# Attention, then a masked convolution: denominators of the last image's last four groups summed by TensorE, and the first pair's preparation moved a slot ahead

## The chip, the cores and the metric

The kernel runs on one core of one Trainium2 chip. The metric is the device time of one execution in microseconds; the median of three runs before the change is 2693.74 us (2692.41 to 2695.08).

## The reference

The input x has 8 images of 512 channels and 32 x 32 positions. Two layers follow one another, each with a residual addition. Cut to what matters:

```
# layer 0: attention, 8 heads per channel split of 64, over the normalised input
q, k, v = t @ Wq.T + bq, t @ Wk.T + bk, t @ Wv.T + bv      # t = group norm of x, as tokens
q, k, v = (a.reshape(B * 8, S, 64) for a in (q, k, v))      # 64 groups of 1024 x 64
attn = softmax(q @ k.T / sqrt(64))
x = x + (attn @ v, back in image form)
# layer 1: a 3x3 convolution behind a mask
xn = group norm of x
mu_x, mu_y = rounded centroids of each channel of xn
m = max(1 - (|posX - mu_x| + |posY - mu_y|) * mask_weight, -1)   # 1 where filter != 1
x = x + conv3x3(max(xn * m, 0), weight) + bias
```

## The kernel before, in words

Each engine has its own program, and the order of its work is written out by hand; semaphores tie the programs together. Work of stage 1 (attention) comes in 64 groups, eight per image. A group has one slot, `slot(img, s)`, and a slot has eight units u. The loops run over image and s; the last image (`more=False`) is written out apart.

In unit u of slot s TensorE (PE) does for the group of this slot four score matmuls (`scores`, L655, into three banks), and for the group of the next slot two or three tiles of maxima (`max_tile`, L630), 16 in a slot and none in units 6 and 7. In units 2, 4, 6, and unit 0 of the next slot, it weighs the values with four kernel chunks' exponentials (`weigh_pair`, L667, fp32, two halves of the array side by side). In slots 0 to 2 it has projections too, which use `qk_bank` in slots 0 and 1. The small tiles go through a ring of three banks (`v_ring`, `take`): a fourth tile waits until VectorE (DVE) has read the first. ScalarE (ACT) takes the exponentials (`exp_tile`, L842, two per unit).

The denominators of a softmax are sums over exponentials. Before the change DVE (`add_tile`, L1150, even tiles) and GpSimd (POOL, `add_tile`, L997, odd tiles) each make seven additions of 128x512 per group, and PE sums the two results over partitions with a matrix of ones (`den_item`, L644 and L646) in unit 2 of the next slot. DVE copies the bank to `den_sb` (L1182); two small transfers, a reciprocal and two more transfers bring back the reciprocals, and POOL multiplies (`divide`, unit 6) and adds the residual (`residual`, unit 7). `exp_tile` waits for the additions that still read its buffer (`sum0`, `sum1`).

Stage 2 (convolution) handles images in four pairs. A pair's input is loaded as four tiles of 128 channels, x 2 images, into two buffers `tile2`, first for moments (`tile_moments`, L181), then again for the normalisation (`norm_tile`, L876) into `r_mem`, which has a zero border. DVE forms row and column sums of eight half tiles (`sums`, L1230 and L1231), tables of the mask (`make_tables`, L1237 to L1271); POOL spreads the tables to a mask (`mask_tile`, L1048) and DVE applies it (`mask_tile`, L1279), alternating between two buffers; ACT clips (`relu`, L884). `make_v` (DVE, L1287 to L1313), `cast_v` (ACT, L890) and `split_v` (DVE, L1324) make the operands of one of six positions; a position's matmuls (L760) are 144. PE begins a position when its `split_v` is done and the filter slabs `u_slab` are loaded.

The preparation of pair 0 lies inside the slots of the last image: moments in slots 2 and 3, the two statistics items (`centre2`, `finish2`, through the ring) in slot 4, the normalisation in slots 4 and 5, sums in slots 5 and 6, tables in slot 6, masks in slots 6 and 7, `make_v(0, 0)` at the end of slot 7. `r_mem` is cleared by one POOL memset in unit 0 of slot 4 (L1060). SyncE (SP) issues all transfers in one queue, in program order.

## Time and profile before

| | |
|---|---|
| median of 3 runs | 2693.74 us |
| the profiled execution, its own time | 2691.37 us |
| span of the profiled execution | 2689.6 us |
| mean granted TensorE clock | 0.984 |
| PE / DVE / ACT / POOL busy | 95% / 77% / 40% / 44% |
| first convolution matmul | 1931.37 us |

The span runs from the first instruction to the last. Busy shares are averages over both stages; the stretch that the change touches lies between some 1660 and 1931 us, where slots 1 to 7 of the last image run. Its slots 3, 4, 5, 6 and 7 begin near 1750, 1775, 1812, 1844 and 1887 us. The clock is a share of 2.4 GHz: 1.00 is that level and 0.50 is 1.2 GHz.

### The profile page before, as it was taken

Reading aid. Unit: us, or ns where it says so; the run is one execution under the profiler, and the core shown is the slowest. Engines: PE = TensorE matmul, PEld = TensorE weight load, DVE = VectorE, ACT = ScalarE, POOL = GpSimd, SP = SyncE. Lnnn points to the kernel's source line nnn. Section 1 sums busy time; section 2 is a strip of 40 time slices with the busy share of each in tenths; the row PEclk is TensorE's granted clock in tenths of the full one; section 3 lists DMA queues with packets and bytes.
Section 4 is the critical chain, followed back from the end, with each engine's and each line's share of the span. In section 5 each row is a group of like instructions: output and inputs, shape, how many; then the busy total and the mean of one; then the engine's idle time right before and its main releaser. Section 6 shows DMA issues by size and latency. Waiting matters only on the chain.

```text
span 2689.6 us, 38766 instructions
## 1 busy us (share of the span) xinstructions
PE 2546.9 (95%) x11312; PEld 998.1 (37%) x11312; DVE 2069.7 (77%) x2832; ACT 1088.5 (40%) x1801; POOL 1170.0 (44%) x907
## 2 busy tenths in 40 slices
PE   5999999999999999999999999976699999999998
PEld 2333333333333333333333333321244444444443
DVE  5887787787788788778878868789868968968614
ACT  3455455455544545544554554443323132122100
POOL 3356466556555655654655564665603003003000
PEclk9999999999999999999999999998799999999999
DMA  5224243241423414324143330531164553744534
GB/s 147 82 74 114 65 125 84 58 133 58 113 83 91 113 45 126 96 65 122 55 118 87 94 107 19 140 100 52 60 230 172 219 203 126 268 155 140 189 107 159
DMA packets 209768, 309.00 MB, mean 115 GB/s; under 512 B 80272, under 2 KB 129552, under 8 KB 209552
## 3 DMA queue, kind: packets, MB, share of 16 engines
q1 hardware_dynamic: 209552, 306.36, 36.8%
q8 instruction: 107, 1.75, 0.3%
q14 instruction: 109, 0.89, 0.1%
HBM read 202.88 MB, written 52.69 MB: 95 GB/s over the span
## 4 chain that ended last, share of the span: by engine, by line
PE 81%; DVE 11%; issue 4%; POOL 2%; ACT 1%; DMA 1%; DVEq 0%; SPq 0%; ACTq 0%; POOLq 0%
PE bank L760 28%; PE bank L667 14%; PE bank L655 13%; PE bank L612 11%; PE bank L630 7%; PE bank L622 5%; DVE nmax L1156 4%; DVE prob_sum L1150 2%; PE bank L644 2%; POOL prob_sum L997 1%; DVE nt L211 1%; DVE rstd L214 1%; DVE nt L209 1%; PE bank L638 1%; ACT prob L842 1%
## 5 line engine op out<-in xcount | busy, mean ns | idle before, releaser
L1156 DVE TENSOR_REDUCE nmax<-bank 128x1 f32<-128x512 f32 x1024 | 660.8, 684 | 213.9 <-PE bank L630 205.2
L842 ACT ACTIVATE prob<-bank 128x512 f32<-128x512 f32 x1024 | 555.9, 596 | 656.2 <-PE bank L655 649.9
L997 POOL TENSOR_TENSOR prob_sum<-prob_sum,prob 128x512 f32<-128x512 f32 x384 | 565.0, 1471 | 448.4 <-ACT prob L842 446.5
L760 PE MATMUL bank<-v,u_slab 128*128 128x512 f16 x3456 | 749.2, 380 | 3.4 <-DVE v L1324 3.4
L667 PE MATMUL bank<-prob,val 128*64 128x512 f32 x2048 | 501.9, 608 | 2.3 <-ACT prob L842 2.3
L760 PEld LDWEIGHTS bank<-v,u_slab 128*128 128x128 f16 x3456 | 338.7, 98 | 412.9 <-DVE v L1324 5.1
L630 PE MATMUL bank<-k_a,q_a 128*128 128x512 f16 x1024 | 389.9, 386 | 39.2 <-DVE nmax L1156 34.4
L1150 DVE TENSOR_TENSOR prob_sum<-prob_sum,prob 128x512 f32<-128x512 f32 x384 | 386.9, 1008 | 13.1 <-DVE shift L1166 8.7
L655 PE MATMUL bank<-q_a,k_a 128*128 128x512 f16 x1024 | 318.1, 385 | 19.0 <-ACT prob L842 16.9
L655 PE MATMUL bank<-q_b,k_b 128*128 128x512 f16 x1024 | 308.8, 384 | 5.4 <-DMA q_b<-shift 5.3
L1048 POOL TENSOR_TENSOR t_a<-tab_mem 128x1224 f32<-128x1224 f32 x16 | 50.1, 3130 | 446.7 <-DVEq L1273 434.4
L667 PEld LDWEIGHTS bank<-prob,val 128*64 128x64 f32 x2048 | 132.1, 137 | 252.0 <-issue 215.3
L630 PEld LDWEIGHTS bank<-k_a,q_a 128*128 128x128 f16 x1024 | 99.9, 98 | 303.4 <-issue 95.2
L612 PE MATMUL bank<-xn_hi,w_hi 128*128 128x512 f16 x512 | 195.3, 381 | 15.0 <-DVE xn_lo L1135 15.0
L997 POOL TENSOR_TENSOR prob_sum<-prob 128x512 f32<-128x512 f32 x64 | 82.3, 1286 | 260.6 <-ACT prob L842 260.3
L612 PE MATMUL bank<-xn_lo,w_hi 128*128 128x512 f16 x512 | 195.3, 381 | 0.0
L612 PE MATMUL bank<-xn_hi,w_lo 128*128 128x512 f16 x512 | 195.1, 381 | 0.0
L830 ACT ACTIVATE qk<-bank,prm 128x512 f32<-128x512 f32 x128 | 88.0, 688 | 229.8 <-PE bank L612 229.8
L655 PEld LDWEIGHTS bank<-q_a,k_a 128*128 128x128 f16 x1024 | 95.3, 98 | 181.6 <-ACT prob L842 73.7
L1003 POOL TENSOR_TENSOR den_sb<-pv_sb,den_sb 128x512 f32<-128x512 f32 x64 | 94.2, 1472 | 123.0 <-DMA den_sb<-recip_scratch 123.0
L655 PEld LDWEIGHTS bank<-q_b,k_b 128*128 128x128 f16 x1024 | 100.2, 99 | 123.6 <-DMA q_b<-shift 10.9
L1142 DVE TENSOR_TENSOR qk_lo<-qk,qk_hi 128x512 f16<-128x512 f32 x128 | 117.4, 917 | 29.6 <-ACT qk_hi L834 13.7
(119 smaller groups left out, 2633.6 us busy)
## 6 DMA issues: line engine op xcount, KB each, us to landing
u_slab<-u_scratch SPq DMA_DIRECT2D x72, 1024.0 KB, 5.0
tile<-x_scratch SPq DMA_DIRECT2D x34, 1024.0 KB, 7.8
xs<-x SPq DMA_DIRECT2D x28, 1024.0 KB, 5.7
u_scratch<-u_w SPq DMA_DIRECT2D x96, 192.0 KB, 2.8
q_a<-qk_hi SPq DMA_DIRECT2D x64, 256.0 KB, 4.8
den_sb<-recip_scratch SPq DMA_DIRECT2D x128, 128.0 KB, 2.9
x_scratch<-xr SPq DMA_DIRECT2D x16, 1024.0 KB, 4.4
xr<-x SPq DMA_DIRECT2D x15, 1024.0 KB, 8.1
```

The source lines that it names most:

```text
L612: mm = pe.matmul(dst[:], a[:, w, c, j * P:(j + 1) * P], b[:, half, c], start=(n == 0), stop=(n == len(steps) - 1))
L622: mm = pe.matmul(dst[:], a[:, half, c, g * TOK:(g + 1) * TOK], b[:, 2, c], start=(n == 0), stop=(n == len(steps) - 1))
L630: pe.matmul(dst[:].rearrange("p (k t) -> p k t", t=TOK), q_a[half][:, m // 2, tok], k_a[half][:, 4 * (m % 2):4 * (m % 2) + 4, tok], start= ...
L655: mm = pe.matmul(sc_bank[b][:].rearrange("p (j t) -> p j t", t=TOK), k_op[half][:, u, tok], q_op[half][:, e, :, tok], start=(part == 0), s ...
L667: pe.matmul(pv_bank[e * D:(e + 1) * D, :], val[s // HPH][:, s % HPH, kc * D:(kc + 1) * D], prob[:, (2 * kc + e) % 8], start=(kc == 0), sto ...
L760: mm = pe.matmul(bank_at(pos, co)[:].rearrange("p (i n) -> p i n", i=2), slab[:, l, c, co * P:(co + 1) * P], image[v][:, 2 * c:2 * c + 2, ...
L842: act.activation(prob[:, (2 * u + e) % 8], sc_bank[bank_turn(s * 16 + 2 * u + e, 16 * HPI)[0]][:], ACT.Exp, scale=float(D) ** -0.5).then_i ...
L997: nc.gpsimd.tensor_tensor(acc, in0, prob[:, (2 * kc + 1) % 8], ALU.add).then_inc(s1["sum1"], 1)
L1003: nc.gpsimd.tensor_tensor(den_sb[:], pv_sb[:], den_sb[:], ALU.mult).then_inc(s1["o_done"], 1)
L1142: dve.tensor_tensor(qk_lo[:, which, j], qk32[:, j % 2], qk_hi[:, which, j], ALU.subtract)\
L1150: dve.tensor_tensor(acc, in0, prob[:, (2 * kc) % 8], ALU.add).then_inc(s1["sum0"], 1)
L1156: dve.tensor_reduce(nmax[:, m // 2, m % 2:m % 2 + 1], src[:], AX.X, ALU.max, negate=True)\
```

## The change

In slots 4 to 7 of the last image the additions on DVE and POOL are left out. In their place `weigh` issues, ahead of the value matmuls of a chunk, two fp32 matmuls with the matrix of ones on the same exponentials, accumulated in `qk_bank`, which the last image does not use after slot 1. DVE copies that bank in unit 2 of the next slot (`den_from_bank`), and the first of these matmuls of a group waits until the copy of the group before is done (`den_out`). `exp_tile` no longer waits for additions there.

The moments move to slots 1 to 3 in the tile order 0, 2, 1, 3 with their loads, the statistics items to slot 3, the normalisation to slots 3 and 4, the sums to slots 4 and 5, tables to slot 5, masks to slots 5 and 6, `make_v(0, 0)` to the end of slot 6. `split_v(0, 0)`, `make_v(0, 1)` and `split_v(0, 1)` move from behind the last slot into slot 7, with the casts. POOL clears only the borders of `r_mem`, with three strided memsets in unit 4 of slot 3.

```
 def stat_units(s, more):
     if more:
         return (4, 6) if s == 1 else ()
-    return (1, 3) if s == 4 else ()
+    return (3, 5) if s == 3 else ()
+
+def den_direct(s, more):
+    return not more and s >= HPH
+FIRST_ORDER = (0, 2, 1, 3)
...
# ring_items: no ("den", 0) where the group before is a direct one
...
# PE
-            def weigh(h, s, kc):
+            def weigh(h, s, kc, direct):
                 if kc == 0:
                     pe.wait_ge(s1["pv_out"], h + 1)
                     pe.wait_ge(s1["value_out"], h + 1)
+                if direct:
+                    if kc == 0:
+                        pe.wait_ge(s1["qk_out"], 1 + 16 * B)
+                        pe.wait_ge(s1["den_out"], h)
+                    pe.wait_ge(s1["exp_done"], 4 + 16 * h + 2 * kc + 2)
+                    for e in range(2):
+                        mm = pe.matmul(qk_bank[e * D:(e + 1) * D, :], ones, prob[:, (2 * kc + e) % 8],
+                                       start=(kc == 0), stop=(kc == SEG - 1))
+                    if kc == SEG - 1:
+                        mm.then_inc(s1["den_full"], 1)
...
-            den_item(B * HPI - 1, 1)
...
# ACT
-                        if s in (4, 5) and u >= 4:
-                            if s == 4 and u == 4:
+                        if s == 3 and u >= 6 or s == 4 and u in (0, 1, 3, 4, 6, 7):
+                            if s == 3 and u == 6:
                                 act.wait_ge(s2["stat2_step"], S2_STEPS)
-                                act.wait_ge(s2["pad_clear"], 1)
-                            norm_tile(0, (s - 4) * 4 + u - 4)
+                                act.wait_ge(s2["pad_clear"], 3)
+                            norm_tile(0, u - 6 if s == 3 else (2, 3, 0, 4, 5, 0, 6, 7)[u])
+                        if s == 5 and u == 7:
+                            relu(0, 0)
+                        if s == 6 and u < 7:
+                            relu(0, u + 1)
                         if s == 6 and u == 7:
                             act.wait_ge(s1["x1_stored"], 16 + 16 * (2 * B - 1))
                             cast_v(0)
+                        if s == 7 and u == 3:
+                            for n in range(3):
+                                act.wait_ge(s1[f"u_out{n}"], 16 + 16 * UQ)
+                            cast_v(1)
...
# POOL
-                        if s == 4 and u == 0:
+                        if s == 3 and u == 4:
                             pool.wait_ge(s1["qk_moved"], 192 * 2 * B)
                             pool.wait_ge(s1["value_out"], B * HPI)
-                            nc.gpsimd.memset(r_mem[:], 0.0).then_inc(s2["pad_clear"], 1)
-                        if s == 6 and u >= 5:
+                            nc.gpsimd.memset(r_row[:, :, TJ:TJ + 1], 0.0).then_inc(s2["pad_clear"], 1)
+                            nc.gpsimd.memset(r_blk[:, :, 0:TJ], 0.0).then_inc(s2["pad_clear"], 1)
+                            nc.gpsimd.memset(r_blk[:, :, BLK - TJ - 1:BLK - 1], 0.0).then_inc(s2["pad_clear"], 1)
+                        if s == 5 and u >= 5:
                             mask_tile(0, u - 5)
-                        if s == 7 and u < 5:
+                        if s == 6 and u < 5:
                             mask_tile(0, u + 3)
-                    if u >= 2:
+                    if u >= 2 and not den_direct(s, more):
                         add_tile(h, s, u - 1)
...
# DVE
+            def den_from_bank(h):
+                dve.wait_ge(s1["den_full"], h - (B * HPI - HPH) + 1)
+                dve.wait_ge(s1["resid_done"], h + 1)
+                dve.tensor_copy(den_sb[:], qk_bank[:]).then_inc(s1["den_out"], 1)
...
+                        if (s, u) in ((1, 1), (2, 1), (2, 5), (3, 1)):
+                            tile_moments(0, FIRST_ORDER[((1, 1), (2, 1), (2, 5), (3, 1)).index((s, u))])
+                        if s == 3 and u == 2:
                             aggregate2()
...
+                        if s == 4 and u in (1, 2, 4, 5, 7) or s == 5 and u < 3:
+                            sums(0, (0, 0, 1, 0, 2, 3, 0, 4)[u] if s == 4 else u + 5)
+                        if s == 5 and u == 4:
                             make_tables()
+                        if s == 5 and u >= 6:
                             mask_tile(0, u - 6)
+                        if s == 6 and u < 6:
                             mask_tile(0, u + 2)
+                        if s == 6 and u == 7:
                             dve.wait_ge(s1["x1_stored"], 16 + 16 * (2 * B - 1))
                             make_v(0, 0)
+                        if s == 7 and u == 1:
+                            split_v(0, 0)
+                        if s == 7 and u == 3:
+                            make_v(0, 1)
+                        if s == 7 and u == 6:
+                            split_v(0, 1)
...
+                        if place == "d" and u == 2 and den_direct(s - 1, more):
+                            den_from_bank(h - 1)
...
-            den_item(B * HPI - 1)
-            split_v(0, 0)
-            make_v(0, 1)
+            den_from_bank(B * HPI - 1)
+            make_v(0, 2)
             invert_sums(B * HPI - 1)
-            split_v(0, 1)
-            make_v(0, 2)
             split_v(0, 2)
```

On SP the tile loads of pair 0 move with the moments: tile 0 in slot 0 and tile 2 in slot 1 behind that slot's reciprocal transfers, tile 1 at the start of slot 2 as before, tile 3 in slot 2 behind the reciprocals, then the second loads of tiles 0 to 3 in slots 3 and 4, one at the start and one behind the reciprocals of each.

## Rows read from the trace of the kernel before

**Rows 1.** Windows: stretch, engines' busy time (instructions), PE clock, DMA share, GB/s

```profile
1750.00:1775.00 25.00, 20.22 (x89) 6.39 (x87) 24.36 (x45) 9.43 (x18) 11.86 (x9) 1.00 0.35 125
1775.00:1812.00 37.00, 25.95 (x92) 8.20 (x91) 26.95 (x51) 19.04 (x28) 25.84 (x20) 0.86 0.16 53
1812.00:1844.00 32.00, 21.43 (x88) 6.54 (x86) 30.55 (x36) 18.98 (x28) 20.37 (x19) 0.95 0.41 134
1844.00:1887.00 43.00, 27.17 (x84) 7.24 (x82) 41.89 (x53) 10.41 (x19) 21.75 (x12) 0.74 0.03 9
1887.00:1923.50 36.50, 20.48 (x64) 5.27 (x62) 33.85 (x18) 17.75 (x24) 34.37 (x14) 0.78 0.26 94
...
1931.40:2677.00 745.60, 745.60 (x3453) 338.55 (x3454) 519.56 (x502) 150.94 (x119) 70.78 (x26) 1.00 0.49 175
```

**Rows 2.** Tiles prob_sum, tab_mem, r_mem, 1700 to 1960 us: ns min/median/max

```profile
L1150 DVE TENSOR_TENSOR prob_sum<-prob_sum,prob x42: 639/889/2852, 1700.0 to 1923.2; 128x512 f32<-128x512 f32 x42
...
L1048 POOL TENSOR_TENSOR t_a<-tab_mem x4: 2362/2811/3554, 1869.1 to 1899.9; 128x1224 f32<-128x1224 f32 x4
...
L1279 DVE SCALAR_TENSOR_TENSOR r_mem<-t_a,r_mem x4: 2494/3038/3587, 1876.0 to 1905.6; 128x1224 f32<-128x1224 f32 x4
...
L1060 POOL MEMSET r_mem<- x1: 8275/8275/8275, 1774.1 to 1774.1; 128x9801 f32 x1
```

**Rows 3.** The chain that ended last, around the first convolution matmul: start, duration

```profile
1928.89 2.43 DVE v L1324
1931.37 28.78 PE bank L760 x122
```

**Rows 4.** Timeline of PE in slots 4 to 7: start, duration, idle before and releaser

```profile
1799.37 0.54 PE L630 MATMUL bank<-k_a,q_a 128*128 128x512 f16 x1 [4.83 <-DVE nmax L1156]
...
1803.64 1.94 PE L667 MATMUL bank<-prob,val 128*64 128x512 f32 x8
...
1882.11 1.04 PE L655 MATMUL bank<-q_b,k_b 128*128 128x512 f16 x2 [2.46 <-DMA q_b<-shift]
1883.08 3.68 PE L667 MATMUL bank<-prob,val 128*64 128x512 f32 x8
```

**Rows 5.** Timeline of DVE in slots 3 to 7: start, duration

```profile
1759.67 2.46 DVE L181 BATCH_NORM_STATS2 bn<-tile 128x6 f32<-128x512 f32 x4
...
1792.01 0.16 DVE L200 SCALAR_TENSOR_TENSOR ve<-bank,gmv 128x8 f32<-128x8 f32 x1
...
1798.54 0.17 DVE L217 SCALAR_TENSOR_TENSOR nbias<-gmv,rstd 128x8 f32<-128x8 f32 x1
...
1823.38 0.68 DVE L1182 COPY den_sb<-bank 128x512 f32<-128x512 f32 x1
...
1844.31 1.42 DVE L1230 TENSOR_REDUCE tab_mem<-r_mem 128x34 f32<-128x1224 f32 x1
1845.64 2.31 DVE L1231 TENSOR_REDUCE tab_mem<-r_mem 128x36 f32<-128x1224 f32 x1
...
1862.84 0.44 DVE L1237 TENSOR_TENSOR tab_mem<-tab_mem,cst 128x272 f32<-128x272 f32 x1
...
1869.07 1.89 DVE L1156 TENSOR_REDUCE nmax<-bank 128x1 f32<-128x512 f32 x3
...
1915.63 2.42 DVE L1287 SCALAR_TENSOR_TENSOR t_a<-r_mem 128x2176 f32<-128x2176 f32 x1
1918.09 3.37 DVE L1287 SCALAR_TENSOR_TENSOR v<-r_mem,t_a 128x2176 f32<-128x2176 f32 x1
```

**Rows 6.** Timeline of POOL in slot 5, first and last of four

```profile
1832.22 1.37 POOL L1026 TENSOR_TENSOR u_w<-u_t,u_w 128x384 f16<-128x384 f32 x1
...
1835.30 1.04 POOL L1031 TENSOR_TENSOR u_t<-u_g 128x192 f32<-128x192 f32 x1
```

**Rows 7.** Page, DMA issues: count, KB each, median us to landing

```profile
u_slab<-u_scratch SPq DMA_DIRECT2D x72, 1024.0 KB, 5.0
tile<-x_scratch SPq DMA_DIRECT2D x34, 1024.0 KB, 7.8
```

More of the change, by code:

```diff
@@ L107, in ring_items @@
         at["d"].append(("den", 0))
+    if prev == "direct":
+        at["d"] = [x for x in at["d"] if x[0] != "den"]
     return at
@@ L168, in build @@
             "u_in", "u_act", "u_pool",
-            "u_out0", "u_out1", "u_out2", "pv_out", "den_out", "den_in", "recip_done", "recip_out", "recip_in", "o_done", "resid_done", "x1_stored", "value_out")}
+            "u_out0", "u_out1", "u_out2", "den_full", "pv_out", "den_out", "den_in", "recip_done", "recip_out", "recip_in", "o_done", "resid_done", "x1_stored", "value_out")}
         def statistics(dve, signal, step, cols):
@@ L411, in load_tile @@
                 if 2 <= n < 6:
-                    sp.wait_ge(s2["stat2_step"], S2_STEPS * pair + 4 * (n - 1))
+                    place = FIRST_ORDER.index(n - 2) if pair == 0 else n - 2
+                    sp.wait_ge(s2["stat2_step"], S2_STEPS * pair + 4 * (place + 1))
                 if n >= 6:
@@ L470, in slot @@
                     load_x(img + 1, 1)
+                if s == 0 and not ahead:
+                    sp.wait_ge(s1["xn_hi"], 8 * B)
+                    sp.wait_ge(s1["x1_stored"], 16 + 16 * 4)
+                    load_tile(0, 0)
+                if not more:
+                    if s == 1:
+                        load_tile(0, 2)
+                    if s == 2:
+                        load_tile(0, 3)
+                    if s == 3:
+                        load_tile(0, 5)
+                    if s == 4:
+                        load_tile(0, 7)
                 if s == 1 and more:
@@ L478, in slot @@
                     store_unit(unit, 1)
-                if s == 2 and not more:
-                    load_tile(0, 2)
-                    load_tile(0, 3)
                 if r == 0 and prev:
@@ L669, in weigh, with weigh_pair @@
                               stop=(kc == SEG - 1)).then_inc(s1["pv_done"], 1)
-            def weigh_pair(h, s, n):
-                weigh(h, s, 2 * n)
-                weigh(h, s, 2 * n + 1)
+            def weigh_pair(h, s, n, direct=False):
+                weigh(h, s, 2 * n, direct)
+                weigh(h, s, 2 * n + 1, direct)
             def slot(img, s, prev=True, nxt=True, more=True):
@@ L681, in slot @@
                 for u in range(UNITS):
-                    items = ring_items(u, nxt, prev, proj and r == 2, stat_units(s, more))
+                    items = ring_items(u, nxt, "direct" if den_direct(s - 1, more) else prev, proj and r == 2,
+                                       stat_units(s, more))
                     def run(place):
@@ L712, in slot @@
                     if u == 0 and prev:
-                        weigh_pair(h - 1, (s - 1) % HPI, SEG // 2 - 1)
+                        weigh_pair(h - 1, (s - 1) % HPI, SEG // 2 - 1, den_direct(s - 1, more))
                     if u >= 2 and u % 2 == 0:
-                        weigh_pair(h, s, u // 2 - 1)
+                        weigh_pair(h, s, u // 2 - 1, den_direct(s, more))
             pe.sem_inc(s1["pv_done"], 8)
@@ L743, in _ @@
                 slot(B - 1, s, nxt=s < HPI - 1, more=False)
-            weigh_pair(B * HPI - 1, HPI - 1, SEG // 2 - 1)
-            den_item(B * HPI - 1, 1)
+            weigh_pair(B * HPI - 1, HPI - 1, SEG // 2 - 1, True)
             def group_sum(pair, k):
@@ L905, in slot @@
                 for u in range(UNITS):
-                    exp_tile(h, s, u, 0)
-                    exp_tile(h, s, u, 1)
+                    added = not den_direct(s - 1 + u // 4, more)
+                    exp_tile(h, s, u, 0, added)
+                    exp_tile(h, s, u, 1, added)
                     if u == 0 and prev:
@@ L958, in _ @@
             evacuate_pv(B * HPI - 1)
-            for n in range(3):
-                act.wait_ge(s1[f"u_out{n}"], 16 + 16 * UQ)
-            cast_v(1)
             act.wait_ge(s1["x1_stored"], 16 + 16 * 2 * B)
@@ L1410, in slot @@
                                 split_norm(img + 1, s // HPH, 3)
-                        if place == "d" and u == 0 and prev:
+                        if place == "d" and u == 0 and prev and not den_direct(s - 1, more):
                             add_tile(h - 1, (s - 1) % HPI, SEG - 1)
-                        if place == "d" and u >= 2:
+                        if place == "d" and u >= 2 and not den_direct(s, more):
                             add_tile(h, s, u - 1)
+                        if place == "d" and u == 2 and den_direct(s - 1, more):
+                            den_from_bank(h - 1)
                         if place == "d" and u in (1, 2) and (s == 0 and ahead or s == 1 and more):
```

36 lines of the change are left out of this document (9 added, 27 removed).

## The prediction

> **What bounds the kernel now.** I read the page for the busy shares first, then the windows cut at the slots of the last image, then the chain of waits around the first convolution matmul, and last the timelines of PE, DVE and POOL between 1750 and 1932 us.
>
> The windows separate two regimes [rows 1]. From 1931.4 to 2677 us PE is busy 745.6 of 745.6 us: the second stage is bound by PE from its first matmul, so the stretch ahead of it decides. There, in slots 3 to 7, DVE is busy 24.4 of 25, 27.0 of 37, 30.6 of 32, 41.9 of 43 and 33.9 of 36.5 us while PE has gaps, and PE's mean clock falls to 0.74 in slot 6. DVE is the bound in slots 5 and 6, DVE and POOL together in slot 7 (POOL 34.4 of 36.5). Slot 4 has 10 us that DVE doesn't fill: the POOL memset of 8.28 us [rows 2] stands ahead of the last addition of slot 3, PE's `den_item` waits for that, and PE does nothing else meanwhile.
>
> The chain shows how the second stage begins [rows 3]: `split_v(0, 0)` takes 2.43 us and ends when the first convolution matmul starts at 1931.37. The next 122 matmuls take 28.78 us. At the pace of the full clock (745.6 us for 3453, 0.216 us each) they would take 26.4, so the start costs 2.4 us at 1.2 GHz.
>
> **Prices.** A `weigh_pair` takes 1.94 us, some 1.85 without the overlap of its end, at the full clock, and 3.68 at the low one [rows 4]. The added matmuls have the same form (fp32, 64 columns, 512 wide, two side by side), so a direct pair costs twice that: 3.7 and 7.4 us. Scores of a unit are 4 x 0.216 = 0.87. A slot's PE work becomes 32 scores and 16 maxima (10.4), four direct pairs (14.8) and a shift, 25.5 us. On DVE [rows 5]: three maxima 1.8 after overlap; half a tile's sums 1.42 + 2.31, 3.6 after overlap; tables 1862.84 to 1869.07, 6.2; the denominators' copy 0.7 to 0.8; a tile's moments 2.4; `finish2` 1792.01 to 1798.7, 6.6, with 16 instructions of which the last takes 0.17, so 2.7 at best and I take 4.5. An addition is 0.64 to 2.85 us, median 0.89 [rows 2].
>
> **The change part by part, as a walk along DVE.** I follow DVE's copy of the denominators in unit 2 of each slot, since in the new version PE and DVE meet there.
>
> *Slots 1 and 2.* One tile's moments (2.4 us) are added to slot 1, two stay in slot 2. The cover is PE's projections; PE is the bound there and I add nothing. Without that cover it is 2.4 us.
>
> *Slot 3.* DVE loses one tile's moments (-2.4) and gets the statistics (+0.6 for the centring, +4.5, between 2.7 and 6.6). The slot's 25 us become 27.7, so slot 4 begins near 1777.7. The border memsets write 1600 of 9801 elements, at memset's pace 1.4 us, as strided ones perhaps 3; POOL has its unit without filter work there. ACT's first normalisation waits for `finish2`, and behind it the exponentials of unit 7, which POOL and DVE then still add: 2 us late, within the slack of slot 4's first unit. The 8.28 us hole is gone.
>
> *Slot 4 to its copy.* Two maxima 1.2, an addition 0.9, two units with sums and three maxima 2 x 5.4, the copy 0.8: 13.7, which ends at 1791.4.
>
> *The new wait.* PE's first ones matmul of a group waits for `den_out`, the copy of the group before. Before, PE weighed while DVE copied. Now the copy must be done; behind the waiting matmul in PE's queue are that direct pair and all maxima of unit 3, for which DVE waits. DVE is idle for 3.7 (a direct pair) + 0.5 (a tile) = 4.2 us in each of slots 4, 5 and 6, unless it has work at the start of unit 3: only slot 6 has (a mask).
>
> *The clock.* PE is idle some 4 us before each such copy (it runs out once the third tile of unit 1 is read, then come 3.6 of sums, 1.8 of maxima, 0.8 of copy, against 1.5 us of PE work). After an idle time of 4.83 us the trace shows slow matmuls [rows 4]: from 1799.37 to 1803.64, 4.3 us for ten matmuls and a small one worth 2.5. So each resumption costs 1.8, at best 0, and 3.7 if the whole pair runs slow as at 1883.08. I take 1.8. The Trainium skill, TensorE: Matmul & The Clock Gate, Part 1, makes the low clock the default, released by activity: by that rule all six resumptions (before units 3 and 6 of slots 4 to 6) would start slow, three more than I count, 5.4 us. No row tells the two apart; slot 5, with waits like these, still had 0.95 [rows 1], and I stay with three.
>
> *Copy 4 to copy 5.* DVE work: six sums 21.8, 16 maxima 9.9, the copy 0.8, small ones 1.1: 33.6. Idle 4.2, clock 1.8, two hand-overs around the shift 1.0: 40.6, ends at 1832.
>
> *Copy 5 to copy 6.* Tables 6.2, maxima 9.9, five masks, copy and small ones 1.4. A DVE mask is 2.5 to 3.6 us, a POOL one 2.4 to 3.6 [rows 2]; with POOL's additions gone I take 2.8: 14. That is 31.5; idle and clock 6.0, hand-overs 1.0. POOL sets the pace of the first masks: `unit_second` stands between masks 0 and 1 with 1832.22 to 1836.34, 4.1 us [rows 6], then `divide` and `residual`: 4 us in which DVE waits. 42.5, ends at 1874.5.
>
> *Copy 6 to the shift of slot 6 (T).* Mask 5 lies in the idle 6.0; then 1.8 + 2.8 + 1.8 + 2.8 + 1.2 + hand-overs and small 1.2 = 11.6; T = 1892.1.
>
> *T to the first convolution matmul.* From here PE is the bound: six direct pairs 22.2, nine units' scores 7.8, together 30.0. `make_v(0, 0)` (2.42 + 3.37, ends at T + 5.6), its cast and `split_v(0, 0)` (T + 10), the copy, and `make_v(0, 1)` (3 x 2.4, T + 18) lie beside it. The cast of `v(0, 1)` stands in ACT ahead of unit 4's exponentials and holds them to T + 20; PE has the direct pair of unit 4 until T + 20. I add 1 us, less 0.7 for the start before T. The slabs are issued behind the reciprocals, which wait for `make_v(0, 1)`: near T + 21, landed 5.0 us later by the median [rows 7]; 8 would still do. First convolution matmul: 1892.1 + 30.3 = 1922.4, against 1931.4: -9.0. PE arrives from 20 us without a gap, so the 2.4 us at the low clock are saved too. What used to stand there (the last additions, `den_item`, `split_v`) is off the path; `den_from_bank(63)` guards only the fourth bank, three times 2.6 us later.
>
> Sum: -11.4 us. The profiled execution took 2691.37 us (span 2689.6), 2.4 less than the median, and would come to 2680.0; against the median, 2693.74 - 11.4 = 2682.3, I say 2682.
>
> Bounds. With masks at 2.4, no clock cost and `finish2` at 2.7 the walk is some 13 us shorter (2669). With masks at 3.6 (+6), `finish2` at 6.6 (+2) and each of three resumptions at 3.7 (+6) it is 14 longer, though these overlap in part (2690).
>
> **Rivals.**
>
> *The wait hides (2667).* If DVE or PE slack covers the copy's wait, 4.2 + 4.2 + 1.4 and the clock costs of 5.4 fall away: -15 more. For: PE has a queue of its own and DVE lags by up to three tiles. Against: `den_out` is in order ahead of the pair, and unit 3 has no DVE work in slots 4 and 5. 0.16.
>
> *Masks exclude each other (2686).* If POOL's mask and DVE's never overlap, each costs 2.4 + 2.4 = 4.8 from the tables on, 38.4 for eight, with POOL's other work 8: 46 against the 42 that I have from the tables to mask 7. +4. The rows show 3.6 beside 2.4, so in part they do. 0.10. The Trainium skill, SBUF — State Buffer, SBUF: two separate sides, has such a lock between a DVE operation with two SBUF inputs and GpSimd; the spread in [rows 2] fits it.
>
> *A transfer late (2686).* Tile 3's second load waits for the reciprocals of slot 4 and lands 7.8 us later [rows 7], close to ACT's unit 6; or the slabs take 10. +4. 0.07.
>
> *The gain is eaten (within 0.2%, 2694).* Clock costs at two places per slot, not one, and at 3.7 each: six times 1.9 more, 11.4. For: the idle before unit 5's minimum is another 4 us. Against: DVE has sums or a mask there. 0.12.
>
> *Slower (2703).* One mechanism: PE stays at 1.2 GHz in slots 6 and 7, where now it is at 0.74 and 0.78. The tail of 30 us is then up to 60. It decides against the change once 11.4 us of that tail's full-clock work run slow; at two thirds, +20, it is 2703. Against: PE has no gap there, and at the convolution's start, without gaps, the slow clock cost 2.4 us and no more. 0.08.
>
> **How the numbers follow.** My forecast, a gain of 11 us, 0.47. Differences within 0.2% (5.4 us) cannot be told from none. Faster: 0.47 + 0.16 + 0.10 + 0.07 = 0.80; same 0.12; slower 0.08. The range 2666 to 2691 takes in the walk's bounds and the hidden wait and leaves the slower case and part of the eaten one out.
>
> **What would show it.** The first L760 matmul near 1922, at the full clock; DVE copies of `qk_bank` near 1791, 1832 and 1874, each followed by 4 to 6 us without DVE work in slots 4 and 5; no prob_sum rows after 1780; PE without a gap over 2 us from slot 6's unit 6 on. Wrong: copies closer than 37 us (the wait hides), PE clock below 0.8 in slots 4 to 7, or a slab wait ahead of L760.

## The result, and the profile after

The changed kernel takes 2685.35 us (median of 10 runs, 2681.84 to 2688.03) against 2694.61 us for the kernel before, measured beside it (10 runs, 2689.03 to 2698.79). The ratio is 0.9969, 95% interval 0.9961 to 0.9977: 8.4 us less (6.2 to 10.5). Below, "us less" is always against the kernel before, and worked out like this: one minus the ratio, times the median of before; differences between two versions are differences of such numbers. The profiled execution took 2683.13 us, with a span of 2681.2 us and a mean granted clock of 0.989.

Windows of the kernel after, cut where DVE begins the sums or masks of each slot and at the first convolution matmul (stretch, busy time of PE, PEld, DVE, ACT, POOL with instructions, PE clock, DMA share, GB/s); they answer to [rows 1]:

```profile
1751.00:1782.50 31.50, 22.69 (x91) 7.34 (x90) 28.39 (x60) 13.05 (x19) 14.22 (x12) 0.89 0.29 98
1782.50:1823.30 40.80, 32.41 (x119) 9.67 (x120) 32.78 (x35) 23.03 (x29) 8.62 (x11) 0.83 0.29 94
1823.30:1860.80 37.50, 28.02 (x115) 8.96 (x114) 25.44 (x43) 12.82 (x25) 16.58 (x13) 0.91 0.07 18
1860.80:1903.00 42.20, 30.44 (x115) 9.39 (x114) 28.91 (x29) 18.62 (x26) 16.71 (x9) 0.84 0.04 12
1903.00:1925.60 22.60, 21.17 (x93) 6.58 (x91) 12.88 (x9) 10.16 (x18) 2.54 (x2) 1.00 0.41 152
1925.60:2670.00 744.40, 744.40 (x3459) 338.49 (x3458) 510.33 (x498) 149.45 (x119) 68.92 (x26) 1.00 0.49 176
```

The stretch from 1660 us to the first convolution matmul is 265.3 us long instead of 271.4. POOL's busy time in it falls from 170.5 to 111.5 us and DVE's from 230.8 to 197.2; PE's grows from 207.6 to 223.7. Ahead of the convolution no engine is full in any window: DVE has 8.0, 12.1 and 13.3 us without work in the second, third and fourth.

Timeline of DVE after, around its copies of the denominators (start, duration, idle time before and what ended it); they answer to the copy in [rows 5]:

```profile
1791.48 0.69 DVE L1212 COPY den_sb<-bank 128x512 f32<-128x512 f32 x1 [0.89 <-PE bank L662]
1797.97 1.99 DVE L1186 TENSOR_REDUCE nmax<-bank 128x1 f32<-128x512 f32 x3 [5.80 <-PE bank L646]
...
1831.85 0.67 DVE L1220 COPY den_sb<-bank 128x512 f32<-128x512 f32 x1
1838.62 1.99 DVE L1186 TENSOR_REDUCE nmax<-bank 128x1 f32<-128x512 f32 x3 [6.10 <-PE bank L646]
...
1874.62 0.68 DVE L1220 COPY den_sb<-bank 128x512 f32<-128x512 f32 x1
1875.22 1.42 DVE L1315 SCALAR_TENSOR_TENSOR r_mem<-t_b,r_mem 128x1224 f32<-128x1224 f32 x1
1882.19 1.99 DVE L1186 TENSOR_REDUCE nmax<-bank 128x1 f32<-128x512 f32 x3 [5.55 <-PE bank L646]
```

Copies at 1791.5, 1831.9 and 1874.6 us, then 5.8, 6.1 and, behind one mask, 5.6 us in which DVE waits for PE's maxima. The next rows show what PE does in the second of these gaps. Timeline of PE after; it answers to [rows 4]:

```profile
1832.78 1.97 PE L687 MATMUL bank<-prob,cst 128*64 128x512 f32 x4 [5.68 <-DVE den_sb L1220]
1834.51 1.95 PE L693 MATMUL bank<-prob,val 128*64 128x512 f32 x4
1836.21 1.19 PE L687 MATMUL bank<-prob,cst 128*64 128x512 f32 x4
1837.22 1.04 PE L693 MATMUL bank<-prob,val 128*64 128x512 f32 x4
...
1841.32 1.08 PE L687 MATMUL bank<-prob,cst 128*64 128x512 f32 x4
1842.23 1.03 PE L693 MATMUL bank<-prob,val 128*64 128x512 f32 x4
```

PE has stood still for 5.68 us until DVE's copy is done, and then eight matmuls, L687 with ones and L693 with values, take 1.97 and 1.95 us per four. From start to start of such a four it is 1.73 us, where the pair from 1841.32 has 0.91 and less: the level of 1.2 GHz. The other eight run at 1.19 and 1.04. This direct pair takes 5.4 us, the next one 3.6. The maxima of unit 3 stand behind it. The pairs behind the other two copies take 5.1 us (slot 4) and 6.2 us (slot 6).

Timeline of ACT and of DVE after, in slot 7 (same columns):

```profile
1900.12 2.02 ACT L917 ACTIVATE v<-v 128x2176 f16<-128x2176 f32 x1 [3.10 <-DVE v L1323]
```

```profile
1894.15 3.42 DVE L1323 SCALAR_TENSOR_TENSOR t_a<-r_mem 128x2176 f32<-128x2176 f32 x1 [2.28 <-ACT r_mem L911]
```

The chain that ended last, after, from slot 7 to the second stage (start, duration, what); it answers to [rows 3]:

```profile
1900.13 0.91 PE bank L693 x4
1901.08 0.96 issue
1902.04 1.06 ACT prob L869 x2
1903.47 0.62 ACT prob L869
1904.13 0.62 PE bank L671 x2
1904.78 0.61 ACT prob L869
1905.45 1.08 PE bank L687 x4
...
1925.35 51.91 PE bank L786 x240
```

DVE's first `make_v(0, 0)` operation waits 2.28 us for the last `relu`; the cast of v(0, 0) waits for it and then holds the exponentials, so that between 1901.08 and 1905.45 the chain runs mainly over ACT. The convolution starts at 1925.3, at the full clock: 240 matmuls in 51.9 us, 0.216 each.

### The profile page after: what moved, and what is told of

It reads as the page before. It is cut to its first block, busy times and chain, and to the rows that moved or that the text cites. A ratio compares the mean times of both kernels' runs of the same rounds, so it can differ in the third digit from the quotient of the medians.

```text
span 2681.2 us, 38876 instructions
## 1 busy us (share of the span) xinstructions
PE 2560.5 (95%) x11424; PEld 1004.8 (37%) x11424; DVE 2030.5 (76%) x2804; ACT 1088.5 (41%) x1801; POOL 1110.8 (41%) x881
## 4 chain that ended last, share of the span: by engine, by line
PE 83%; DVE 11%; issue 3%; ACT 1%; POOL 1%; DMA 0%; DVEq 0%; SPq 0%; ACTq 0%
PE bank L786 28%; PE bank L693 15%; PE bank L671 13%; PE bank L628 11%; PE bank L646 7%; PE bank L638 5%; DVE nmax L1186 3%; PE bank L660 2%; DVE prob_sum L1180 2%; PE bank L687 1%; ACT prob L869 1%; DVE nt L219 1%; DVE rstd L224 1%; PE bank L654 1%; DVE nt L221 1%
## 5 line engine op out<-in xcount | busy, mean ns | idle before, releaser
L786 PE MATMUL bank<-v,u_slab 128*128 128x512 f16 x3456 | 746.9, 379 | 0.0
L1026 POOL TENSOR_TENSOR prob_sum<-prob_sum,prob 128x512 f32<-128x512 f32 x360 | 526.0, 1461 | 419.4 <-ACT prob L869 417.9
L693 PE MATMUL bank<-prob,val 128*64 128x512 f32 x2048 | 499.8, 606 | 0.0
L1180 DVE TENSOR_TENSOR prob_sum<-prob_sum,prob 128x512 f32<-128x512 f32 x360 | 358.9, 997 | 12.0 <-DVE shift L1196 8.9
L693 PEld LDWEIGHTS bank<-prob,val 128*64 128x64 f32 x2048 | 132.7, 137 | 252.0 <-issue 219.3
L1026 POOL TENSOR_TENSOR prob_sum<-prob 128x512 f32<-128x512 f32 x60 | 76.0, 1267 | 258.5 <-ACT prob L869 258.2
L1032 POOL TENSOR_TENSOR den_sb<-pv_sb,den_sb 128x512 f32<-128x512 f32 x64 | 88.6, 1384 | 151.7 <-DMA den_sb<-recip_scratch 151.7
```

The source lines that it names most:

```text
L693: pe.matmul(pv_bank[e * D:(e + 1) * D, :], val[s // HPH][:, s % HPH, kc * D:(kc + 1) * D], prob[:, (2 * kc + e) % 8], start=(kc == 0), sto ...
L786: mm = pe.matmul(bank_at(pos, co)[:].rearrange("p (i n) -> p i n", i=2), slab[:, l, c, co * P:(co + 1) * P], image[v][:, 2 * c:2 * c + 2, ...
L1026: nc.gpsimd.tensor_tensor(acc, in0, prob[:, (2 * kc + 1) % 8], ALU.add).then_inc(s1["sum1"], 1)
L1032: nc.gpsimd.tensor_tensor(den_sb[:], pv_sb[:], den_sb[:], ALU.mult).then_inc(s1["o_done"], 1)
L1180: dve.tensor_tensor(acc, in0, prob[:, (2 * kc) % 8], ALU.add).then_inc(s1["sum0"], 1)
```

## The experiments

The versions were measured in three groups, four to eleven runs of each, every group on a chip of its own and beside its own runs of the kernel before, whose medians were 2693.82 us (e1 to e4), 2694.05 us (e5 to e8) and 2694.06 us (e9 to e11). Brackets hold the 95% interval of a ratio; its half is 3 to 4 us for most versions, so a difference of less than some 5 us between two versions is not shown by the ratios alone.

**e1: only the borders.** The kernel before, with the three small memsets in the old place (the view `r_blk` that they use is added too).

```
-                                act.wait_ge(s2["pad_clear"], 1)
+                                act.wait_ge(s2["pad_clear"], 3)
...
-                            nc.gpsimd.memset(r_mem[:], 0.0).then_inc(s2["pad_clear"], 1)
+                            nc.gpsimd.memset(r_row[:, :, TJ:TJ + 1], 0.0).then_inc(s2["pad_clear"], 1)
+                            nc.gpsimd.memset(r_blk[:, :, 0:TJ], 0.0).then_inc(s2["pad_clear"], 1)
+                            nc.gpsimd.memset(r_blk[:, :, BLK - TJ - 1:BLK - 1], 0.0).then_inc(s2["pad_clear"], 1)
```

> The kernel before, with only the POOL clearing of r_mem changed to the three border memsets, still in unit 0 of slot 4. Theory (the hole behind the 8.28 us memset is one term of the gain, and DVE is the bound from there on, so what is won there is kept): the three memsets take some 3 us, DVE's wait of 5.8 us in slot 4 falls below 1, the first convolution matmul comes 4 to 5.5 us sooner, near 1926.5, total -4 to -5.5 us. Rival 1 (the whole gain of the change is this): -8. Rival 2 (given back in slots 5 to 7, where POOL sets the pace of the masks): within 2 us of before.

Measured: 2684.31 us, ratio 0.9970 [0.9958, 0.9982], 8.1 us less, as much as the whole change. In the kernel before DVE's first copy in slot 4 stood at 1785.65 behind 5.76 us without work; here it has no gap. Timeline of DVE in e1:

```profile
1780.94 0.68 DVE L1185 COPY den_sb<-bank 128x512 f32<-128x512 f32 x1
```

The memset of 8.28 us [rows 2] was not hidden: this one edit alone is worth 8 us. I had expected 4 to 5.5. The number is that of the first rival, though e3 shows that it is not the whole of what the change can gain.

**e2: only the preparation, moved, with the borders.** The changed kernel with its additions kept on DVE and POOL.

```
 def den_direct(s, more):
-    return not more and s >= HPH
+    return False
...
-            weigh_pair(B * HPI - 1, HPI - 1, SEG // 2 - 1, True)
+            weigh_pair(B * HPI - 1, HPI - 1, SEG // 2 - 1)
+            den_item(B * HPI - 1, 1)
```

(and the last addition and `den_item` on POOL and DVE as before.)

> The changed kernel with the additions on DVE and POOL kept in the last four groups (no matmuls with the ones there, denominators as before): preparation a slot sooner and border memsets alone. Theory (the additions and the copy's wait cost about the same in slots 4 to 6, and what the additions would cost more lies in the last slot): without the copy's wait but with some 6.5 us of additions per slot on DVE, first convolution matmul 1922 to 1932, total -10 to 0. Rival (the additions removed are what pays, the move alone does nothing or harm): +2 to +10.

Measured: 2696.19 us, ratio 1.0006 [0.9996, 1.0016], 1.6 us more, with zero inside the interval; I had expected 0 to 10 less, and the rival, 2 to 10 more, is nearer. Against e1, which has the borders too, the move costs some 10 us. DVE waits 2.60, 2.26 and 2.25 us for POOL's masks, which now share slots 5 and 6 with the additions.

**e3: only the denominators.** The kernel before with `den_direct`, the ones matmuls, `den_from_bank` and the skipped additions exactly as in the diff of the change, and nothing moved.

> The kernel before with only the denominators of the last four groups summed by PE, preparation and full memset where they were. Theory: slots 4 to 6 gain 6.5 us of DVE work each and lose 6 to the copy's wait; slot 7 and the end lose additions on POOL and DVE (POOL 34.4 of 36.5 us there) and gain PE work; first convolution matmul 1912 to 1925, total -6 to -18. Rival (PE work added is on the path): 0 or slower.

Measured: 2678.19 us, ratio 0.9948 [0.9934, 0.9961], 14.0 us less, inside what was expected. The memset's hole is still there (DVE idle 6.49 us before its first copy in slot 4), and so is the new wait (6.10 us behind it).

**e4: the copy a unit sooner, in slots 5 to 7.**

```
-                        if place == "d" and u == 2 and den_direct(s - 1, more):
+                        if place == "d" and u == 1 and den_direct(s - 1, more):
```

> The changed kernel with DVE's copy of the direct denominators in unit 1 of slots 5 to 7 and not in unit 2; slot 4 is as it was. Theory (the first ones matmul of a group waits for a copy that stands behind unit 2's sums or mask and maxima, and DVE then idles 5.8 to 6.1 us): the idle stretches of DVE behind the copies of slots 5 and 6 (6.1 and 5.6 us) shrink to under 2, the one of slot 4 (5.8) stays; 8 to 11 us less than the changed kernel, -16 to -20 against before. Rival 1 (POOL's masks and filter work set the pace of slots 5 and 6 anyway): 0 to 3 us less than the changed kernel. Rival 2 (PE becomes the bound): 3 to 6 less.

Measured: 2673.64 us, ratio 0.9922 [0.9908, 0.9935], 21.0 us less, 12.6 less than the changed kernel, somewhat more than the 8 to 11 expected. Timeline of DVE in e4:

```profile
1794.39 0.69 DVE L1212 COPY den_sb<-bank 128x512 f32<-128x512 f32 x1 [0.89 <-PE bank L662]
1800.80 1.99 DVE L1186 TENSOR_REDUCE nmax<-bank 128x1 f32<-128x512 f32 x3 [5.72 <-PE bank L646]
...
1829.01 0.70 DVE L1220 COPY den_sb<-bank 128x512 f32<-128x512 f32 x1
...
1867.21 0.67 DVE L1220 COPY den_sb<-bank 128x512 f32<-128x512 f32 x1
1867.81 1.42 DVE L1315 SCALAR_TENSOR_TENSOR r_mem<-t_a,r_mem 128x1224 f32<-128x1224 f32 x1
```

In slot 4, where the copy wasn't moved, the idle time behind it stays 5.72 us. In slots 5 and 6 DVE goes on at once with sums or a mask. So taking away the wait that the prediction named gives the time back.

**e5: the denominators and the borders, nothing moved** (the edits of e3 and e1 together).

> The kernel before with PE's denominators and the border memsets, the preparation left in its old slots: the change without its move. Theory (the move costs: borders alone gave 0.9970, PE's denominators alone 0.9948, the whole change only 0.9969): the two terms add, -18 to -23 us against before, first convolution matmul 1908 to 1914. Rival (both terms empty the same hole, or the tail's POOL and ACT work, which the move takes off the end, bounds this version): -12 to -16.

Measured: 2671.36 us, ratio 0.9917 [0.9904, 0.9930], 22.4 us less. The two parts add up (8.1 + 14.0 = 22.1). The whole change differs from e5 only by the move, and stands 14.0 us behind it. DVE still waits for PE's maxima here: 4.27 us in slot 4, 3.66 and 2.82 in slot 5, 3.37 in slot 6.

**e6: e5 with all four copies in unit 1** (the edit of e4; in slot 4 `ring_items` places `("den", 0)` in unit 1 too).

> As the run with PE's denominators and borders in the old slots, and the denominators' copies of slots 4 to 7 in unit 1 in place of unit 2. Theory (DVE idles 2.5 to 6 us behind each copy in slots 4 to 6): 6 to 12 us less than without the earlier copy, -26 to -33 against before. Rival (slots 6 and 7 are bound by POOL, which waits for reciprocals between the masks, so only slots 4 and 5 gain): 2 to 6 us less.

Measured: 2667.85 us, ratio 0.9905 [0.9890, 0.9919], 25.6 us less, 3.2 less than e5 (its slowest run, 2668.04 us, is below the fastest of e5, 2669.80). The rival's number held, and behind slot 6's shift DVE does wait for POOL's masks (3.49, 2.26 and 2.26 us) and for the last `relu` (6.13 us). Its reason held in part only: from shift to shift, slot 4 takes 24.6 us instead of 24.9, slot 5 33.3 instead of 34.7 and slot 6 35.5 instead of 39.1, so most of the gain lies in slot 6.

**e7: half the ones matmuls.** The denominators of the last four groups sum only the odd kernel chunks' exponentials.

```
-                    for e in range(2):
+                    for e in range(2) if kc % 2 else ():
...
-                                       start=(kc == 0), stop=(kc == SEG - 1))
+                                       start=(kc == 1), stop=(kc == SEG - 1))
```

> The changed kernel with the ones matmuls of every second chunk left out (denominators sum only half of the exponentials; all else as it was): a direct pair is 1.8 us shorter at the full clock. Theory (PE's pair is on the path behind each copy and throughout slot 7, hidden elsewhere): three waits of DVE behind the copies shrink from 5.6 to 6.1 to some 3.5 to 4 us, six pairs of the tail save up to 11 us less what ACT holds: 12 to 16 us less than the changed kernel. Rival (PE's added work is hidden behind DVE and ACT): under 5 us less.

Measured: 2680.58 us, ratio 0.9953 [0.9940, 0.9965], 12.7 us less, only 4.3 less than the changed kernel, where 12 to 16 were expected. My theory of this run fell. Timeline of PE in e7, behind the copy of slot 5:

```profile
1833.20 1.98 PE L693 MATMUL bank<-prob,val 128*64 128x512 f32 x4 [5.79 <-DVE den_sb L1220]
1834.93 1.95 PE L687 MATMUL bank<-prob,cst 128*64 128x512 f32 x4
1836.64 1.95 PE L693 MATMUL bank<-prob,val 128*64 128x512 f32 x4
```

The pair has twelve matmuls instead of sixteen, and takes 5.3 us instead of 5.4: all twelve run at the low level. In this trace the clock takes what the missing matmuls save in slots 4 and 5, and DVE's gaps stay at 5.77 and 6.16 us. In slot 6 the pair takes 4.5 us instead of 6.2, and the gap 3.94 instead of 5.55. In slot 7 six pairs save 5.2 us, but from the shift (1889.49) to the first convolution matmul (1921.80) it is 32.3 us, only 1.4 less than in the changed kernel. The rest goes into waits for exponentials, the longest of them behind the first cast, with slow matmuls after it. Timeline of PE in e7:

```profile
1900.85 0.61 PE L671 MATMUL bank<-q_a,k_a 128*128 128x512 f16 x1 [3.35 <-ACT prob L869]
```

**e8: all four copies in unit 1, preparation moved** (e4 and, in slot 4, the item as in e6).

```
-    if prev and u == 2:
+    if prev and u == (1 if prev == "early" else 2):
...
-  ... "direct" if den_direct(s - 1, more) else prev, ...
+  ... "direct" if den_direct(s - 1, more) else "early" if s == HPH and not more else prev, ...
```

> The changed kernel with the copy in unit 1 in slots 5 to 7 (as in the fourth run) and, new, the last ring item for denominators and its copy in unit 1 of slot 4 too. Theory (the idle 5.7 us behind the copy of slot 4 has the same cause): it falls below 2, 4 to 5 us less than the fourth run, -24 to -27 against before. Rival (slot 4 waits for ACT's normalisations or the sums instead): under 1.5 us less.

Measured: 2667.95 us, ratio 0.9905 [0.9891, 0.9920], 25.6 us less, 17.2 less than the changed kernel and 4.6 less than e4, both as expected. No gap over 0.25 us stands behind a copy; the shift of slot 6 is at 1873.71 instead of 1891.59; from there to the first convolution matmul it is 33.7 us in both. From 1660 us to that matmul DVE is without work for 50.2 us instead of 68.1, and PE's clock is 0.96 instead of 0.92.

**e9: the tail reordered.** The changed kernel with the casts of slot 7 a unit later.

```
-                        if s == 6 and u == 7:
+                        if s == 7 and u == 1:
                             act.wait_ge(s1["x1_stored"], 16 + 16 * (2 * B - 1))
                             cast_v(0)
-                        if s == 7 and u == 3:
+                        if s == 7 and u == 4:
...
-                        if s == 7 and u == 1:
-                            split_v(0, 0)
                         if s == 7 and u == 3:
+                            split_v(0, 0)
                             make_v(0, 1)
```

> The changed kernel with only its tail reordered: the cast of v(0, 0) on ACT one unit later in slot 7 (behind unit 1's exponentials), split_v(0, 0) on DVE in unit 3 ahead of make_v(0, 1), the cast of v(0, 1) behind unit 4's exponentials. Theory: from the shift of slot 6 to the first convolution matmul the changed kernel took 33.7 us where 30.3 were predicted, and 2.3 of the 3.4 us are PE's waits of 1.36, 0.42 and 0.50 us for exponentials that stand in ACT's queue behind the cast of v(0, 0), which waits 3.10 us for make_v. With the cast later these go: 2 to 2.5 us less than the changed kernel, about -10.5 us against the kernel before, and the stretch is 31.4 us. Rival: ACT is the bound of the tail whatever the order, and the waits only move behind the later cast: 0 to 0.5 us less, -8.3.

Measured: 2684.70 us, ratio 0.9964 [0.9951, 0.9978], 9.7 us less: not told apart from the changed kernel. The trace says more. Timeline of PE in e9:

```profile
1915.00 0.51 PE L671 MATMUL bank<-q_a,k_a 128*128 128x512 f16 x1 [3.16 <-ACT prob L869]
1915.29 1.06 PE L671 MATMUL bank<-q_b,k_b 128*128 128x512 f16 x2
1916.29 1.98 PE L687 MATMUL bank<-prob,cst 128*64 128x512 f32 x4
```

The waits of 1.36, 0.42 and 0.50 us are gone, and one of 3.16 us stands in their place, behind the second cast; after it PE runs eight matmuls slow. From the shift (1889.56) to the convolution (1925.53) it is 36.0 us, 2.3 more than in the changed kernel. My theory of the mending fell: the waits move, as the rival said, and cost more in the new place.

The shift itself is 2.0 us sooner than in the changed kernel, though no edit stands ahead of it. The pair behind the copy in slot 6 is the cause. Timeline of PE, first in the changed kernel, then in e9:

```profile
1875.55 1.98 PE L687 MATMUL bank<-prob,cst 128*64 128x512 f32 x4 [2.55 <-DVE den_sb L1220]
```

```profile
1876.14 1.08 PE L687 MATMUL bank<-prob,cst 128*64 128x512 f32 x4 [2.55 <-DVE den_sb L1220]
```

Both come behind the same two waits, 5.67 and 2.55 us, and the same matmuls. In one execution the pair starts slow and takes 6.2 us, in the other it runs at the full clock and takes 3.6. So the clock's part of a wait differs from execution to execution, and one trace of each version prices it only roughly.

**e10: the same tail in e8.**

> The same reordering of the tail in the version whose copies of the denominators stand in unit 1 of all four slots (-25.6 us). Its stretch from the shift to the first convolution matmul is 33.7 us too, so the theory gives again 2 to 2.5 us less: -27.5 to -28.5 us. Rival (waits only move): -25.6.

Measured: 2671.68 us, ratio 0.9916 [0.9902, 0.9929], 22.6 us less, 3.0 more than e8. The stretch behind the shift is 37.2 us (1876.62 to 1913.85), with a wait of 3.15 us behind the second cast. Wrong again, by the same mechanism in the trace; the lowest of its five runs (2670.66 us) lies above the highest of e8 (2668.47), though e8 is of another group.

**e11: e10 with POOL's mask 1 ahead of `unit_second`.**

```
                         if u == 5:
+                            if s == 5 and not more:
+                                mask_tile(0, 1)
                             unit_second(q)
```

(and not again in unit 6.)

> The kernel of e10 with POOL's mask 1 ahead of unit_second in slot 5 instead of behind it. Two readings of DVE's wait of 3.16 us at mask 1: (a) POOL sets the pace from the tables to mask 3 (in the version with copies in unit 1 POOL has no idle time from 1834.1 to 1855.3 us), so the wait at mask 1 goes and comes back at masks 2 and 3: 0 to 1 us less than e10; (b) DVE's order sets the pace and the 3.16 us are a loss of their own: 2.5 to 3.5 us less than e10. I hold (a) likelier, since POOL's list of work is unchanged.

Measured: 2672.58 us, ratio 0.9912 [0.9898, 0.9926], 23.7 us less, 1.1 less than e10 by the ratios and within its error. Timeline of DVE in e11:

```profile
1845.56 1.42 DVE L1317 SCALAR_TENSOR_TENSOR r_mem<-t_a,r_mem 128x1224 f32<-128x1224 f32 x1
...
1847.32 1.73 DVE L1317 SCALAR_TENSOR_TENSOR r_mem<-t_b,r_mem 128x1224 f32<-128x1224 f32 x1
1854.30 2.48 DVE L1317 SCALAR_TENSOR_TENSOR r_mem<-t_a,r_mem 128x1224 f32<-128x1224 f32 x1 [5.25 <-POOL t_a L1077]
```

The wait at mask 1 (3.16 us) is gone and comes back at mask 2, 5.25 us instead of 2.27. From the shift of slot 5 to that of slot 6 it is 34.0 us instead of 35.0. So reading (a) held: POOL's list of work sets most of this stretch.

## Why the prediction was right, and where it was off

2682 was said and 2685.35 came; the walk gave 11.4 us and 8.4 were measured. Of the profiled execution, 2680.0 was worked out and 2683.1 came. The mechanism of the new wait was right and is shown. That the sum came so near is in part luck, since misses inside it cancelled, as told below. The lower bound was drawn wide without a reason: its own terms (masks 3.2, clock 5.4, `finish2` 1.8) make 10.4 us, not 13.

**The walk to T held, to a microsecond.** Copies at 1791.4, 1832 and 1874.5 were said; 1791.5, 1831.9 and 1874.6 came. T was 1892.1 and came at 1891.6. The new wait was sized at 4.2 us and 1.8 of clock: the gaps of 5.8 and 6.1 us are just that, mostly the pair (5.1 and 5.4 us). e4 and e8 show that it is the cause and not only a neighbour: with the copy one unit sooner the gaps go, and with them 12.6 us (three slots' copies) and 17.2 us (all four).

**The clock: four slow restarts of a pair.** The prediction counted three at 1.8 us, 5.4 in all. The three pairs behind the copies are slow, and cost 1.5, 1.8 and 2.6 us over the 3.6 of a fast one, 6.0 in all. There is a fourth: before unit 6 of slot 4 PE starts at 1810.6 after 3.51 us without work, and the first three groups of four take 1.97, 1.92 and 1.75 us. It cost the walk nothing, since DVE had sums to do meanwhile: between the copies of slots 4 and 5 DVE is without work for 7.1 us in all, and 7.0 were said. Before unit 6 of slots 5 and 6 the waits are 0.43 us or none, and nothing runs slow. The Trainium skill, TensorE: Matmul & The Clock Gate, Part 1, has the low clock as the default that activity releases; as I read it, the prediction would have had six by that rule. The trace agrees on the fourth, and in slots 5 and 6 there was no such wait right before unit 6. Slow matmuls stand outside the counted places too: at 1777.4 behind 5.80 us without work and at 1869.8 behind 5.67, while at 1847.5, behind 2.52 us, they run at the full clock.

**Slot 3 was longer by another part than I said.** `finish2` was to take 4.5 us and took 6.4. Timeline of DVE after, three of its steps while POOL divides, adds and adds the residual (1770.68 to 1774.38 us):

```profile
1770.69 1.27 DVE L224 SCALAR_TENSOR_TENSOR rstd<-nt,rstd 128x8 f32<-128x8 f32 x1
1772.00 1.18 DVE L219 TENSOR_TENSOR nt<-rstd 128x8 f32<-128x8 f32 x1
1773.21 1.19 DVE L221 SCALAR_TENSOR_TENSOR nt<-nt,ve 128x8 f32<-128x8 f32 x1
```

ACT's first normalisation waits 7.06 us for it, the exponentials stand behind, and PE is without work for 5.8 us until 1777.4. PE still takes up slot 4's scores about where I had the slot's begin (1777.7), and the copy comes where I had it, so the slack that I claimed in slot 4's first unit was there, but it was used up.

**The masks: right sum, wrong parts.** From the tables to mask 7 I had 42 us (the walk's own terms give 43.7), and 42.0 came (1846.7 to 1888.7), but DVE's masks were to cost 2.8 each and its waits for POOL 4 us in all. Tile r_mem after, with `mask_tile`'s DVE operation (L1315) and the border memsets (ns min/median/max); they answer to [rows 2]:

```profile
L1315 DVE SCALAR_TENSOR_TENSOR r_mem<-t_a,r_mem x4: 1421/1714/2481, 1850.5 to 1884.1; 128x1224 f32<-128x1224 f32 x4
L1315 DVE SCALAR_TENSOR_TENSOR r_mem<-t_b,r_mem x4: 1386/1952/3581, 1855.2 to 1887.3; 128x1224 f32<-128x1224 f32 x4
...
L1089 POOL MEMSET r_mem<- x1: 2073/2073/2073, 1757.3 to 1757.3; 128x1088 f32 x1
L1090 POOL MEMSET r_mem<- x1: 396/396/396, 1759.2 to 1759.2; 128x256 f32 x1
L1091 POOL MEMSET r_mem<- x1: 358/358/358, 1759.5 to 1759.5; 128x256 f32 x1
```

DVE waits 3.16, 2.27 and 1.92 us at masks 1 to 3, 7.4 in all, and its eight masks take 16.2 us (both rows, all eight added up), not 22.4. These two misses, 3.4 us more and 6.2 less, cancel in part; 1.0 more went into slot 6, where copy 6's gap with its mask took 7.0 us and not 6.0. That the copies and T came to a microsecond is in this part luck. The borders took 2.8 us and lay where POOL had room, as said.

**The tail was the mis-sized term.** T to the first convolution matmul was predicted at 30.3 us and took 33.7; with T 0.5 us sooner than said, this leaves the 2.9 us between 1922.4 and 1925.3. By the timeline of PE, its parts are: six direct pairs of 3.6 us, 21.5 (I had 22.2); nine units' scores of 1.0 to 1.1, 9.2 (I had 7.8, four times 0.216 without what lies between a score and a pair); waits for exponentials, 3.1 (I had 1.0); and the start, which I had put 0.7 before T and which lay 0.1 before it. Of the waits 2.3 us are the 1.36, 0.42 and 0.50 behind the first cast, since `make_v(0, 0)` began at T + 2.6 behind the last `relu`, and not at T; 0.8 are three of 0.26, one of them beside the second cast, which cost nothing more. e9 and e10 show that putting the casts later doesn't mend this: a cast of 2 us that waits for DVE in ACT's queue holds PE in both places that were tried, and after the wait of 3.16 us the matmuls are slow too. In e7 six direct pairs have 5.2 us less, and the stretch is only 1.4 us shorter (32.3): once PE has less to do, it waits for ACT's exponentials instead. So PE's list of work alone, by which the prediction priced the tail, does not set it; the cast is close behind. The start at the full clock saved 2.3 us (746.9 us for the convolution's matmuls against 749.2), 2.4 were said.

**The rivals.** That the wait hides fell (gaps as sized). That masks exclude each other was right as a fact and wrong as a price, 3.8 us for the two together and not 4.8 (below). The second load of tile 3 was late, as that rival said: ACT waited 7.2 us for it at 1815.6, and nothing in the traces followed from it. The clock ate 0.6 us more than counted behind the copies, not 11. PE did not stay at 1.2 GHz: the clock is 0.84 in the window of slot 6 and 1.00 in the one after it.

**What the prediction did not see.** It took the change as one. Its three parts are worth -8.1 us (borders), -14.0 (denominators) and about +10 without and +14 with the denominators (the move), the last the difference of e5 and the whole. I had the move as a gain, since it takes the preparation off the end. The traces show where it costs. Against e5, the shift comes 4.2 us later in slot 3, which must bring the statistics first, 15.2 in slot 4, 21.1 in slot 5 and 21.8 in slot 6; the tail, with its work done sooner, gives 7.8 back, which leaves 14.0. With the copies in unit 1 (e8 against e6) it is 5.1, 9.9, 11.7 and 10.7, and the first convolution matmul is only 2.0 us later. In e6 the convolution's matmuls then take 749.6 us instead of 746.9, so the moved and the unmoved version are equal (both 25.6 us less). So some 12 of the 14 us depend on where the copy stands. Up to the first convolution matmul DVE is without work for 68.1 us in the changed kernel and 58.7 in e5, and for 50.2 and 50.1 in e8 and e6. Why the copy's wait costs so much more in the moved order is argued and not shown: no DVE work is left for the unit after the copy in slots 4 and 5, but the single gaps (5.8, 6.1 and 5.6 us against 4.3, 3.7, 2.8 and 3.4 in e5) account for 3.3 us only. Nor is it settled what the moved order would be worth if POOL had the masks' waits off its way: e6 and e8 come out equal with different waits, at the masks and the last `relu` in e6, in the tail in e8.

The best two versions, e6 and e8, are 25.6 us faster than before, three times the change.

## What to carry to other kernels

Take a compound change apart before you believe its sum: here one part alone gave as much as the whole change, and another gave back more than half of what the rest had won. When a buffer is handed from one group to the next by a copy on another engine, put the copy at the head of that engine's work for the slot, and keep independent work of that engine for right behind it; here that was worth 12.6 to 17.2 us in the moved order, but only 3.2 in the unmoved one. Price a wait of a few microseconds ahead of TensorE with its slow restart, as a range and not as one number.

## What the runs showed of the hardware that I had not expected

A DVE mask (two SBUF inputs) takes 1.39 to 1.42 us when no POOL operation holds it up (four of the eight in the changed kernel). The others end that much later than the POOL operation beside which they started. Timeline of POOL after, then of DVE:

```profile
1856.40 3.56 POOL L1077 TENSOR_TENSOR t_a<-tab_mem 128x1224 f32<-128x1224 f32 x1
...
1865.53 2.35 POOL L1077 TENSOR_TENSOR t_a<-tab_mem 128x1224 f32<-128x1224 f32 x1
```

```profile
1855.24 2.48 DVE L1315 SCALAR_TENSOR_TENSOR r_mem<-t_b,r_mem 128x1224 f32<-128x1224 f32 x1 [3.16 <-POOL t_b L1077]
1859.99 2.48 DVE L1315 SCALAR_TENSOR_TENSOR r_mem<-t_a,r_mem 128x1224 f32<-128x1224 f32 x1 [2.27 <-POOL t_a L1077]
...
1865.60 3.58 DVE L1315 SCALAR_TENSOR_TENSOR r_mem<-t_b,r_mem 128x1224 f32<-128x1224 f32 x1 [1.92 <-POOL t_b L1077]
```

POOL's mask ends at 1865.53 + 2.35 = 1867.88, and DVE's, started at 1865.60, ends at 1869.18, 1.30 later. The same for 1855.24 + 2.48 = 1857.72 behind POOL's 1856.43, and 1859.99 + 2.48 = 1862.47 behind 1861.19: 1.29 and 1.28 later. So the durations of 2.5 to 3.6 us here are waits for POOL plus a mask of 1.3 to 1.4. It is the same in the kernel before: the mask at 1875.95 ends at 1878.44, 1.28 us after POOL's addition. I had read the durations in [rows 2] as the cost of a mask. POOL's 3.56 us at 1856.40 is the same from the other side: it ends at 1859.96, 2.24 us after DVE's mask of 1855.24. The Trainium skill, SBUF — State Buffer, SBUF: two separate sides, has this as an exclusive lock; the trace agrees, and gives its price: the sum of both, 3.8 us for a mask of each. Even the 8-element steps of `finish2` with two SBUF inputs show it: 1.2 us each while POOL was running, 0.17 otherwise, and each ends 0.02 us after POOL's operation.

The second was e7: behind 5.7 to 5.8 us without work a pair of sixteen matmuls took 5.4 us, eight of them slow, and a pair of twelve 5.3 us, all of them slow. In that trace, what was taken out of the pair came back as clock. But in slot 6 the pair of twelve was the faster one, by 1.7 us, and there the same sixteen matmuls behind the same waits took 6.2 us in one execution and 3.6 in another (e9). So the slow stretch behind a wait is no fixed number of matmuls, and no fixed time either. No run here varied the idle time alone.
